# Attention with a small expert layer on one core: keys projected in the first stretch, output products in the second or third

## The reference

```python
xn = _layer_norm(x, ln_g, ln_b)
q = (xn @ wq + bq) ...          # the same for k and v, 16 heads of 64
scores = jnp.einsum('bhqd,bhkd->bhqk', q, k) / jnp.sqrt(jnp.float32(D))
mask = jnp.tril(jnp.ones((S, S), bool), k=-1)
scores = jnp.where(mask, NEG_INF, scores)
a = jax.nn.softmax(scores, axis=-1)
h = jnp.einsum('bhqk,bhkd->bhqd', a, v)
return h @ w0 + b0 + residual
```

## Time and profile before

| | us |
|---|---|
| median of three runs | 1002.89 |
| lowest and highest | 1001.41, 1004.12 |
| the profiled execution | 1005.35 |
| its span, first to last instruction | 1003.5 |
| TensorE matmuls busy | 963.6 (96%) |
| TensorE weight loads busy | 603.8 (60%) |
| VectorE busy | 645.9 (64%) |
| ScalarE busy | 538.0 (54%) |
| GpSimd busy | 703.1 (70%) |
| mean granted TensorE clock | 0.993 |

### The profile page before, as it was taken

One profiled execution on the slowest core, in us unless ns is written; L12 is line 12 of the kernel. 1 busy time (PEld: TensorE's weight loads), 2 busy tenths in 40 slices (PEclk: granted clock), 3 DMA queues, 4 the chain that ended last, 5 costly groups with the idle time before them and its releaser, 6 DMA issues.

```text
span 1003.5 us, 20485 instructions
## 1 busy us (share of the span) xinstructions
PE 963.6 (96%) x7677; PEld 603.8 (60%) x7682; DVE 645.9 (64%) x1935; ACT 538.0 (54%) x732; POOL 703.1 (70%) x519
## 2 busy tenths in 40 slices
PE   8999999999999999999999999999999999999995
PEld 3465666666666665666665566566666656666563
DVE  4766566565567667657667757656665765756377
ACT  6245655564544565665455565565545546455443
POOL 7266767687666768876576977776687776777752
PEclk9899999999999999999999999999999999999999
DMA  4001101001111100012001210000101210000010
GB/s 114 22 2 24 23 2 23 24 23 44 23 23 26 20 23 23 23 23 45 17 8 23 65 24 23 23 17 8 44 22 24 64 24 14 12 23 23 23 44 21
DMA packets 61809, 26.94 MB, mean 27 GB/s; under 512 B 39056, under 2 KB 53776, under 8 KB 61712
## 3 DMA queue, kind: packets, MB, share of 16 engines
q1 hardware_dynamic: 61712, 25.64, 10.9%
HBM read 22.76 MB, written 2.35 MB: 25 GB/s over the span
## 4 chain that ended last, share of the span: by engine, by line
PE 75%; POOL 11%; DVE 6%; ACT 5%; issue 3%; DMA 0%; POOLq 0%; ACTq 0%; DVEq 0%
PE po L698 21%; PE st L683 15%; PE st L614 9%; POOL total L467 8%; PE sc L649 8%; PE st L761 5%; PE st L678 5%; ACT ring L969 3%; PE sc L708 3%; PE st L629 2%; DVE sc L1156 2%; PE st L630 1%; PE st L631 1%; POOL moments L438 1%; DVE stats L1129 1%
## 5 line engine op out<-in xcount | busy, mean ns | idle before, releaser
L467 POOL TENSOR_TENSOR total<-total,ring 128x1024 f32<-128x1024 f32 (+1 forms) x313 | 539.4, 1723 | 251.6 <-PE po L698 208.6
L1156 DVE CUSTOM_DVE_ANT_0 sc<-sc,key_mask 128x512 f32<-128x512 f32 (+1 forms) x496 | 230.3, 521 | 144.8 <-PE sc L649 142.4
L969 ACT ACTIVATE ring<-st 128x1024 f32<-128x1024 f32 (+1 forms) x256 | 228.7, 919 | 166.3 <-PE st L683 148.3
L1159 DVE TENSOR_REDUCE least<-sc 128x1 f32<-128x512 f32 x268 | 170.2, 677 | 74.6 <-PE sc L649 70.6
L698 PE MATMUL po<-ring,v_sb 128*64 128x512 f32 (+3 forms) x1280 | 210.7, 467 | 0.0
L683 PE MATMUL st<-q_high,k_low 64*128 64x512 f32 (+3 forms) x768 | 177.0, 447 | 0.0
L698 PEld LDWEIGHTS po<-ring,v_sb 128*64 128x64 f32 x1280 | 86.7, 137 | 129.2 <-issue 124.1
L649 PE MATMUL sc<-k_high,q_high 64*128 64x512 f32 (+3 forms) x768 | 135.3, 383 | 11.3 <-DVE least L1156 5.2
L683 PE MATMUL st<-q_low,k_high 64*128 64x512 f32 (+3 forms) x768 | 136.9, 343 | 0.0
L683 PE MATMUL st<-q_high,k_high 64*128 64x512 f32 (+3 forms) x768 | 136.3, 342 | 0.0
L649 PEld LDWEIGHTS sc<-k_high,q_high 64*128 64x128 f32 x768 | 68.8, 185 | 82.4 <-issue 65.9
(11 more groups left out here) (170 smaller groups left out, 1281.2 us busy)
## 6 DMA issues: line engine op xcount, KB each, us to landing
inv_row<-sums_dram SPq DMA_DIRECT2D x62, 256.0 KB, 4.0
x_a<-x SPq DMA_DIRECT2D x4, 512.0 KB, 5.2
sums<-sums_row SPq DMA_DIRECT2D x124, 2.0 KB, 2.1
x_b<-x SPq DMA_DIRECT2D x3, 512.0 KB, 5.5
out<-res_b SPq DMA_DIRECT2D x3, 512.0 KB, 4.5
ring<-w_pairs SPq DMA_DIRECT2D x1, 1152.0 KB, 7.3
shift_row<-shift_t SPq DMA_DIRECT2D x64, 4.0 KB
x_a<-x SPq DMA_DIRECT2D x2, 256.0 KB, 3.2
```

What stands on the lines that cost most here:

```text
L467: nc.gpsimd.tensor_tensor(so_far, so_far, tile_of(n, s)[:, :, col:col + w], ALU.add).then_inc(s_add, 1)
L969: nc.scalar.activation(tile_of(n, s)[:, :, 0:w], st[s % 2][:, :, 0:w], ACT.Exp, scale=SCALE).then_inc(s_exp, 1)
L1156: last = nc.vector.tensor_tensor_reduce(bank[:, col:col + w], bank[:, col:col + w], key_mask[:, 0:w], -1.0, 3e38, ALU.add, ALU.min, least[ ...
L1159: last = nc.vector.tensor_reduce(least[:, h, a:a + 1], bank[:, col:col + w], AX.X, ALU.max, negate=True)
```

## The change

Only the plan of the fills and what goes with it is changed:
- `k(t+2)` moves from the second stretch (bank `x`) to the first (bank `y`, behind `q`).
- `out(t-2)` moves from the first stretch to the third (bank `y`, behind `v`); in pairs 1, 5 and 6 to the second stretch (bank `y`, as the first fill). In the last slot it stays in the first stretch, in bank `x`.
- `u` and `mix` (second stretch of pairs 5 and 6) go from bank `y` to bank `x`.
- The second layer norm's statistics on `acc` move one place later (places 5 and 6), and the roots that need them from stretch (2, 0) to (2, 1).

```diff
         x, y = ((1, 0), (1, 0), (0, 1))[g]
-        if t + 2 < N:
-            found.append(((("q", t + 2, 0), ("k", t + 2, 0), ("v", (t + 2) // 2, t % 2))[g], x))
+        if g == 0 and t + 2 < N:
+            found += [(("q", t + 2, 0), x), (("k", t + 2, 0), y)]
+        if g == 2 and t + 2 < N:
+            found.append((("v", (t + 2) // 2, t % 2), x))
+        if g == (1 if i in (1, 5, 6) else 2) and 2 <= t < N - 1:
+            found.append((("out", t - 2, 0), y))
         if g == 0:
-            if 2 <= t < N:
-                found.append((("out", t - 2, 0), y))
+            if t == N - 1:
+                found.append((("out", t - 2, 0), x))
             if 1 <= t < N:
                 found.insert(0, (("sum", t - 1, 0), "sc"))
...
         if after and (i, g) == (5, 1):
-            found.append((("u", c - 1, 0), y))
+            found.append((("u", c - 1, 0), x))
...
         if after and (i, g) == (6, 1):
-            found.append((("mix", c - 1, 0), y))
+            found.append((("mix", c - 1, 0), x))
...
-    ROOT_TIMES = [(1, 1, 0, 1), (2, 0, 2, 0), (3, 2, 1, 1), (4, 1, 3, 0), (7, 2, 4, 0)]
+    ROOT_TIMES = [(1, 1, 0, 1), (2, 1, 2, 0), (3, 2, 1, 1), (4, 1, 3, 0), (7, 2, 4, 0)]
...
             def after_scores(b, place):
 
-                if place == 4:
+                if place == 5:
                     wait_taken(dve, "out", PAIRS * (b + 1) - 1, 0)
                     norm_stats(2, acc[b % 2], low)
-                elif place == 5:
+                elif place == 6:
                     norm_stats(2, acc[b % 2], high).then_inc(s_var, 1)
```

## The result

The changed kernel takes 1037.9 us in the median of six runs (1033.94 to 1041.23); the kernel before took 1002.65 in six runs beside it. The ratio is 1.0348, with an interval of 1.032 to 1.0375. The forecast was 1030.8 with a range of 1016 to 1040. The profiled execution after took 1035.33 us with a span of 1033.5, so it is 30.0 us longer than the one before (1003.5) and 2.6 us short of the median.

What follows compares the result with a forecast made beforehand. TensorE was taken to bound the kernel, so each wait it gets adds time. Waits and relief of +22.8 plus clock falls of +5.1 on the profiled 1005.35 gave 1033.3, less 2.46 a median of 1030.8 us, range 1016 to 1040.

Steps and rivals of the forecast that it cites:

- `normalise` waits for `out`: Third stretch, 18 slots: GpSimd's `normalise` waits for `out`, delaying TensorE's sum; +4.3, +11.8 and +5.5 us, slot 1 +1.4.
- The last exponential: Second stretch, pairs 1, 5, 6: `out` comes first and TensorE waits for ScalarE; ten new waits of 0.85, +8.5 us.
- Waits that go: k_low's wait after the second stretch goes in slots 9 and 17, -1.3 us; VectorE's scaling step runs free, -1.7.
- The collision of slot 16: VectorE's small scaling step took 2.20 us beside GpSimd's `add_res`; it was to come earlier and run free, -1.7 us.
- Moved and hidden: k's fill in the first stretch, VectorE's take of `out`, the moved roots and SP's spreading were all to cost 0.
- Seams: One projection lead-in saved in each of 18 slots, between 0 and 0.3 us, taken as 0.1: -1.9 us.
- some waits of VectorE that I price at 0: Given, with every clock fall at 1.7 us, as the reason for the range's top of 1040 us.
- The clock: After long TensorE waits the granted clock falls to 0.50; three falls at 1.7 us each, +5.1, ends 0 and 24.
- three of seven: Of seven new waits of 2.35 and 2.76 us, three followed by a clock fall, as dense products stand on both sides.
- The sum: All terms: +22.8 us of waits and relief plus +5.1 for the clock, giving 1033.3 profiled and 1030.8 in the median.
- The rival with a fall at every long wait: Clock falls at all seven long waits: 1037.6 us at 1.7 each, 1049.5 at 3.4 each; chance 0.06.

Runs made afterwards that it cites:

- Experiment 1: Changed kernel with two buffers for o_norm, so `normalise` waits for an `out` one slot older: 1012.73 us, 1.0076 of the kernel before.
- Experiment 2: Changed kernel with `out` ahead of v in the third stretch, their banks swapped: 1016.93 us, 1.0116 of the kernel before.
- Experiment 7: Kernel before with only `out` moved to the third stretch in the same 18 slots, keys left in the second: 1027.96 us, ratio 1.0224.
- Experiment 3: Changed kernel with `out` of pairs 1, 5, 6 in the bank free first, `u` and `mix` in the other: 1025.82 us, ratio 1.0213.
- experiment 8: Changed kernel with two o_norm buffers, `out` of pairs 1, 5, 6 in the bank free first, slot 30's `out` in the first stretch: 996.74 us, ratio 0.9929.
- experiment 6: Changed kernel with slot 30's `out` kept in the first stretch, bank y: 1031.9 us, 1.0265 of the kernel before.
- the changed kernel's second profile: Changed kernel itself, nothing altered, run once more on the second chip: 1037.76 us, 1.033 of the kernel before.
- experiment 5: Changed kernel rerun on another chip (1037.76 us), then with 9 or 11 products of zeros ahead of the sum in the seven long waits: 1030.16 us.

## Why the prediction was right, point by point

- **`normalise` waits for `out`: right in place and size.** 18 waits, as counted. A plain slot waits 0.38 idle, 0.41 to 0.45 from start to start, where 0.39 was forecast; slots with `roots_of` 2.23 idle (forecast 2.35 from start to start), with `add_res` 2.67 (2.76), slot 1 1.40 (1.4). Experiments 1, 2 and 7 show the cause: a second buffer removes it, an earlier `out` shortens it by as much, and `out`'s move alone makes it.
- **The last exponential: right.** 8.9 us in 11 fills, ten of them new, against +8.5. Experiment 3 removes them.
- **Waits that go: right.** k_low's is gone. In slot 11 the score product waits for the maxima instead, 1.3 us where about 1.15 was said. The collision of slot 16 is gone (0.17 for 2.20). The Trainium skill's rule that GpSimd and some VectorE instructions exclude each other for a whole instruction ("SBUF — State Buffer", "SBUF: two separate sides") agrees with the trace at both ends: a small step was freed in slot 16 and two were caught in slot 30.
- **Moved and hidden: right for k in its new place and for VectorE's take of `out`.** No wait for either is in the list.
- **Seams: too small.** 0.1 us a slot was taken, and 0.2 came (28.41 + 0.41 - 28.61 = 0.21; 28.41 - 28.19 = 0.22 in experiment 8). In 18 slots that is about 4 us in favour where 1.9 was forecast, inside the bounds given.
- **Missed: slot 30.** The step of the prediction that failed is "what is moved and hidden". It asked what covers the work that was moved, and not what starts earlier where a stretch is left without any fill. Slot 30 has neither q nor k, so with `out` gone GpSimd's additions follow the sum 2 us sooner and meet VectorE's gate steps. It cost 5.6 us, some 3.3 by the wait and 2.3 by the fall behind it (an estimate from the groups of products there); experiment 6 gives back 5.9. The reason for the top of the range, "some waits of VectorE that I price at 0", names this kind of cost, but not the place.
- **The clock: right in kind, its size partly luck.** In the profiled execution falls cost about 5.5 us by the lengths of the groups in them (1.6 in each of slots 20 and 24, right behind the waits, and 2.3 in slot 30, where TensorE waited through part of it), against 5.1. The sizes agree by luck: the seven waits had two falls and not three, and the last 2.3 are slot 30's. The median lies 2.6 us above that execution; the changed kernel's second profile shows five falls at the seven waits, and experiment 5 puts the term at 7.6 us in the median, on another chip. The fall at 969.1 in the kernel before is not in this profile, and little hangs on it: from the last sum to the end it is 52.5 us here and 52.7 before. The reason given for three of seven, dense products on both sides, was not tested.
- **The sum.** Forecast +27.9 for the profile, measured +30.0: the seams gave 2 more than forecast, slot 30 took 3.3 that were missed beside the clock, and the rest is tenths. For the median +28.1 was forecast and 35.3 measured. Of these 7.2, 5.0 come from where the profiled executions stand among the runs: the forecast took the changed kernel's to be 2.46 above its median, as before, and it is 2.6 below. The granted clocks of the six runs fit this (0.987 in the profiled one, 0.982 and 0.986 in the two about the median). The rival with a fall at every long wait gave 1037.6, next to the 1037.9 measured; that is chance, since no profile shows seven falls there, and slot 30 makes up the difference.

## What to carry to other kernels

A fill that moves later does not only need cover for itself: look for whoever waits for its completion to overwrite its input, and then for what is queued behind that wait. Here waits of up to 2.4 us on an engine with idle time to spare became 0.4 to 2.7 us on the engine that bounds the kernel, because the additions for the next sum stood behind them. One more buffer took the wait away, one place earlier in the order most of it, and the plan of the change, with three cures, then beat the kernel before by 0.7%. And where work leaves a stretch, look at what starts sooner there: in slot 30 that cost 5.6 us.

## What the runs showed of the hardware

Idle time on TensorE cost more than its length. The changed kernel's profile, its second one and those of experiments 3, 6 and 7 have the same seven waits of 2.2 to 2.7 us, and 2, 5, 3, 5 and 2 of these were met by a stretch at a granted clock of 0.50, 3.4 us long (6.8 in one case). The wait of slot 23 was met by one in all five, that of slot 16 in none and that of slot 24, as long as slot 16's, in two (experiments 3 and 6); what decides it is not explained. With 9 to 11 products of zeros in the same waits no fall followed. The runs of the change lay 7.3 us apart on the first chip and 2.7 on the second, those with the zeros 1.9. And a VectorE step on eight columns that takes 0.17 us alone took 2.1 to 2.3 us when it started within 0.3 us after the start of a GpSimd addition, ending with it.
